# Layer 2's routing and row stores beside its attention, row loads beside layer 3, and layer 3 as a pipeline over batches

## What is computed

```python
# layer 2, ffn: a switch layer (8 experts, capacity 256 of 4096 tokens)
probs = softmax(x @ w_switch + b_switch);  pmax, routes = probs.max(-1), probs.argmax(-1)
oh = (routes[:, None] == arange(E));       pos = (cumsum(oh, axis=0) * oh).sum(-1) - 1
keep = pos < capacity;                     slot = where(keep, routes * capacity + pos, E * capacity)
buf = zeros(...).at[slot].set(x)
y = relu(buf_e @ w1 + b1) @ w2 + b2
out = where(keep, y[slot], x) * (pmax / stop_gradient(pmax))
# layer 3, attn: a selective state-space scan (16 states), then layernorm and a projection
delta = softplus(x @ W_delta.T);  B, C = x @ W_B.T, x @ W_C.T;  A = -exp(A_log)
h = h * exp(delta_t * A) + (delta_t * x_t) * B_t;   y_t = sum_n h * C_t
ctx = (layernorm(y) * gamma + beta) @ W_ctx.T * scale
# layer 3, ffn: 8 gated experts with the best 2 of 8, and 2 shared ones
```

## Time and profile before

| what | value |
|---|---|
| runs | 3924.53, 3929.08 and 3936.21 us, median 3929.08 |
| profiled execution | 3926.07 us, its span 3924.7 us |
| PE busy | 2991.2 us, 76% |
| DVE busy | 2349.8 us, 60% |
| ACT, POOL busy | 1477.4 and 814.9 us |
| mean granted PE clock | 0.8 of full speed |
| layer 2's attention ends at | 3075.0 us |
| layer 3 begins at about | 3242 us |

### The profile page before, as it was taken

The page is one execution under the profiler, slowest core; times in us unless marked ns, Lnnn a source line. Parts: engine busy times, 40 slices in busy tenths (PEclk is TensorE's granted clock), DMA queues, the critical chain, the costliest instruction groups (busy, mean ns, idle before and its releaser), DMA issues.

```text
span 3924.7 us, 47435 instructions
## 1 busy us (share of the span) xinstructions
PE 2991.2 (76%) x18187; PEld 2107.0 (54%) x18187; DVE 2349.8 (60%) x4533; ACT 1477.4 (38%) x3673; POOL 814.9 (21%) x468
## 2 busy tenths in 40 slices
PE   4877776777775869999999999688888246676676
PEld 2555454555543756666666666456555134444444
DVE  3587787788677235656566666333333217777776
ACT  1333443443343004545545454233323014444444
POOL 0032223222234201222222222100000331221221
PEclk9788888888887657989998999676677567787787
DMA  1000010001000420000000000100000030000000
GB/s 47 18 33 33 23 34 33 23 23 39 28 33 33 138 73 1 1 1 1 1 1 1 1 1 1 39 7 4 6 6 5 22 85 3 3 3 5 3 3 5
DMA packets 55346, 80.35 MB, mean 20 GB/s; under 512 B 4688, under 2 KB 38480, under 8 KB 54608
## 3 DMA queue, kind: packets, MB, share of 16 engines
q1 hardware_dynamic: 50896, 72.07, 5.6%
q0 software_dynamic: 2048, 4.20, 0.3%
q10 hardware_dynamic: 2176, 1.05, 0.1%
HBM read 68.12 MB, written 8.65 MB: 20 GB/s over the span
## 4 chain that ended last, share of the span: by engine, by line
PE 52%; DVE 29%; ACT 6%; POOL 5%; issue 5%; DMA 1%; POOLq 1%; SPq 0%; DVEq 0%; ACTq 0%
DVE h L1289 7%; PE psum L415 5%; PE psum L455 5%; PE psum L282 4%; DVE mx L1174 3%; PE psum L523 3%; PE psum L527 3%; DVE h L1281 3%; PE psum L435 2%; PE psum L683 2%; POOL h L2047 2%; PE psum L722 2%; PE psum L643 2%; POOL h L2036 2%; PE psum L534 2%
## 5 line engine op out<-in xcount | busy, mean ns | idle before, releaser
L2047 POOL TENSOR_TENSOR h<-h,Crep 128x1024 f32<-128x1024 f32 x128 | 352.9, 2763 | 947.1 <-DVE h L1289 947.1
L2017 POOL TENSOR_TENSOR pr<-pr,rsum 128x512 f32<-128x512 f32 x192 | 241.9, 1260 | 937.6 <-DVE rsum L1131 937.6
L1289 DVE TENSOR_TENSOR_SCAN h<-dA,h 128x1024 f32<-128x1024 f32 x128 | 363.6, 2845 | 0.7
L1774 ACT ACTIVATE pt<-psum 128x1024 f32<-128x1024 f32 x192 | 190.2, 1019 | 434.0 <-PE psum L534 434.0
L683 PE MATMUL psum<-h,pack_wf 128*128 128x256 f32 x1024 | 293.8, 442 | 56.7 <-POOL h L2047 56.7
L1174 DVE TENSOR_REDUCE mx<-psum 128x4 f32<-128x1024 f32 (+1 forms) x192 | 225.2, 1213 | 104.9 <-PE psum L532 104.9
L683 PEld LDWEIGHTS psum<-h,pack_wf 128*128 128x128 f32 x1024 | 223.6, 228 | 112.2 <-POOL h L2047 68.3
L1731 ACT ACTIVATE pr<-psum,nb 128x256 f32<-128x256 f32 (+1 forms) x512 | 208.4, 417 | 170.3 <-DVE nb L1123 169.6
L2036 POOL TENSOR_TENSOR h<-h,Crep 128x1024 f32<-128x1024 f32 x64 | 150.9, 2358 | 522.6 <-DVE h L1366 522.6
L415 PE MATMUL psum<-kT,qT 64*128 64x256 f32 (+1 forms) x1024 | 249.1, 381 | 3.3 <-ACT pr L1731 3.3
L1281 DVE TENSOR_TENSOR h<-dtu,psum 128x512 f32<-128x512 f32 x256 | 163.6, 679 | 105.6 <-PE psum L695 105.6
(11 more groups left out here) (338 smaller groups left out, 5984.7 us busy)
## 6 DMA issues: line engine op xcount, KB each, us to landing
Crep<-c_rows SPq DMA_DIRECT2D x64, 512.0 KB, 3.7
w1r<-m_w SPq DMA_DIRECT2D x32, 256.0 KB, 3.2
w2r<-m_w SPq DMA_DIRECT2D x32, 256.0 KB, 3.0
pack_wf<-wf SPq DMA_DIRECT2D x1, 3192.0 KB, 10.5
slots<-xn SPq DMA_DIRECT2D x16, 128.0 KB, 1.8
w1s<-s_w SPq DMA_DIRECT2D x8, 256.0 KB, 2.6
w2s<-s_w SPq DMA_DIRECT2D x8, 256.0 KB, 3.1
out<-X SPq DMA_DIRECT2D x16, 128.0 KB, 1.8
```

The lines of the kernel that those rows point to most:

```text
L1289: ve.e.tensor_tensor_scan(flat(h), flat(k.dA[c][r]), flat(h), 0.0, ALU.mult, ALU.add).then_inc(*k.set("scanned", 0, b, g, c))
L2017: po.e.tensor_tensor(p3, p3, bcast(k.rsum[u % 3][:, 0:len(heads)], P * (q + 1), 2), ALU.mult).then_inc(*k.set("normed", l, b, u))
L2047: po.e.tensor_tensor(h[:, :, :], h[:, :, :], k.Crep[n % 3][:, :, :], ALU.mult).then_inc(*k.set("hC", 0, b, g, c))
```

## The change

Layer 2:
- `slots` is zeroed by 12 DMAs at the start of layer 1 (before: 4 DMAs for the experts' part at the start of layer 2, and own rows by 16 stores). `po_pre2` and `sp_own_rows` are gone.
- The routing is part of `ve_pre2`, batch by batch, with the running totals in `run`; two small matmuls of the one-hot matrix are put at slot 21 of `pe_pre2`. Its small instructions work on 2 tiles instead of 32.
- POOL stores the rows of a batch (2 indirect DMAs) as soon as its slots are known.
- All 8 experts have weight and row buffers of their own, loaded ahead; PE runs the first matmuls of expert e before the second of e-1.
- The rows are loaded in layer 3, 2 indirect DMAs a batch, two turns ahead, and added in `ve_pre3` by one scaled add for each tile.

Layer 3 is a pipeline of 18 turns. Turn t has `inner` and `moe` of batch t, the four scan groups (`states`) of batch t-1, `post` of batch t-2 and `pre` of batch t+1. B and C are stored as 32 rows in DRAM (`bc_rows`) and spread by 8 DMAs of 512 KB a batch into one `Brep` and one `Crep` buffer for each group; the split, PE's spreading, and ACT's copies of C are gone. DVE makes `dtu*B` as one instruction of 1024 columns from SBUF.

```diff
+def pe_inner3(k, b):
+    pe, w, xnT = k.pe, k.w, k.xnT[b % 2]
+    yield 0
+    bk = pe_take(k, 3)
     pe.wait_ge(*k.at("xnT", 3, b))
+    pe.e.matmul(bk[0:2 * NS, 0:L], w["w_bc3"], xnT[:, :], start=True, stop=True)
+    pe.e.matmul(bk[:, L:2 * L], w["w_delta"], xnT[:, :], start=True, stop=True).then_inc(*k.set("dt", 3, b))
+def pe_states3(k, b):
+    for g in range(4):
+        yield STATES_AT[g] + 9
+        pe.wait_ge(*k.at("hC", 3, b, g))
...
+        for n in range(NG):
+            i = pe.e.matmul(bk, k.w["ident"], k.h[g][:, n, :], start=g == 0 and n == 0, stop=g == 3 and n == NG - 1)
+    yield 21
+    bk = pe_take(k, 2)
+    pe.wait_ge(*k.at("onehot", b))
+    pe.e.matmul(bk[:, 0:QT * E2], w["upto"], k.ohb[:, :], start=True, stop=True)
+    pe.e.matmul(bk[:, QT * E2:2 * QT * E2], w["onesb"], k.ohb[:, :], start=True, stop=True).then_inc(*k.set("totals", b))
+def ve_inner3(k, b):
+    yield 1.5
+    ve.wait_ge(*k.at("dt", 3, b))
+    ve.e.tensor_copy(k.bcrow[b % 2][:, :], bk[0:2 * NS, 0:L]).then_inc(*k.set("crow", 3, b))
...
+def ve_states3(k, b):
+    for g in range(4):
+        at, h = STATES_AT[g], k.h[g]
+        yield at
+        ve.wait_ge(*k.at("dtu", 3, b))
+        ve.wait_ge(*k.at(f"b_spread{g}", b))
+        if b:
+            ve.wait_ge(*k.at("summed", 3, b - 1, g))
+        ve.e.tensor_tensor(h[:, :, :], bcast(k.dtu[b % 2][:, :], NG, 1), k.Brep[g][:, :, :], ALU.mult).then_inc(*k.set("dbu", 3, b, g))
+        yield at + 1.5
+        ve.wait_ge(*k.at("dA", 3, b, g))
+        ve.wait_ge(*k.at("dbu", 3, b, g))
+        ve.e.tensor_tensor_scan(flat(h), flat(k.dA[g][:, :, :]), flat(h), 0.0, ALU.mult, ALU.add).then_inc(*k.set("scanned", 3, b, g))
 def ve_pre3(k, b):
+    ve.wait_ge(*k.at(f"gathered{b % 3}", b))
+    for q in range(QT):
+        n, x = b * QT + q, k.X[:, b * QT + q, :]
+        i = ve.e.scalar_tensor_tensor(x, k.got[b % 3][:, q, :], k.scl[:, n:n + 1], x, ALU.mult, ALU.add)
+def po_states3(k, b):
     po = k.po
+    for g in range(4):
+        po.wait_ge(*k.at("scanned", 3, b, g))
+        po.wait_ge(*k.at(f"c_spread{g}", "states3", b))
+        po.e.tensor_tensor(k.h[g][:, :, :], k.h[g][:, :, :], k.Crep[g][:, :, :], ALU.mult).then_inc(*k.set("hC", 3, b, g))
+def sp_spread3(k, b, g):
+    sp.wait_ge(*k.at(f"c_stored{b % 2}", 3, b))
+    for n, (t, name) in enumerate(((k.Brep[g], f"b_spread{g}"), (k.Crep[g], f"c_spread{g}"))):
+        if b:
+            sp.wait_ge(*(k.at("hC", 3, b - 1, g) if n else k.at("dbu", 3, b - 1, g)))
+        rows = bcast(k.bc_rows[b % 2, n * NS + g * NG:n * NS + (g + 1) * NG, :], P, 0)
+        sp.e.dma_start(t[:, :, :], rows).then_inc(*(k.set(name, "states3", b, by=16) if n else k.set(name, b, by=16)))
...
+def turn3(k, t, pre, inner, moe, states, post):
+    T = TURN[3]
+    merge((post(k, t - 2), 0, T, T) if post is not None and 0 <= t - 2 < NB else None,
+          (states(k, t - 1), 0, T, T) if 0 <= t - 1 < NB else None,
+          (inner(k, t), 0, T, T) if inner is not None and t < NB else None,
+          (moe(k, t), 0, T, T) if moe is not None and t < NB else None,
+          (pre(k, t + 1), 0, T, T) if pre is not None and t + 1 < NB else None)
```

More of the change, by code:

```diff
@@ new lines, in pe_moe @@
+def pe_moe(k, b):
+    pe, w, xnT, B = k.pe, k.w, k.xnT[b % 2], k.bank
+    for q in range(QT):
+        at = EXPERTS_AT[q]
+        was = (b, 0) if q else (b - 1, 1) if b else None
+        yield at
+        xl = xnT[:, q * P:(q + 1) * P]
+        pe.wait_ge(*k.at("xnT", 3, b))
+        if was is not None:
+            pe.wait_ge(*k.at("hs_up", *was))
+            pe.wait_ge(*k.at("hT3", *was))
+        for wt, bk, tail in (("x_w1", B[0], B[2][:, 0:P]), ("x_w3", B[1], B[5][:, 0:P])):
+            pe.e.matmul(bk[:, :], xl, w[wt][:, 0:512], start=True, stop=True)
+            pe.e.matmul(tail, xl, w[wt][:, 512:], start=True, stop=True).then_inc(*k.set("w13", b, q, wt))
+        yield at + 12
+        pe.wait_ge(*k.at("hs", b, q))
+        for ch in range(5):
+            o = B[0][:, ch * P:(ch + 1) * P] if ch < 4 else B[2][:, 0:P]
+            i = pe.e.transpose(o, k.hs[:, ch * P:(ch + 1) * P], w["ident"])
+        i.then_inc(*k.set("hs_turned", b, q))
+        yield at + 15
+        pe.wait_ge(*k.at("hT3", b, q))
+        if was is not None:
+            pe.wait_ge(*k.at("x_moe", *was))
+        for ch in range(5):
+            i = pe.e.matmul(B[6][:, 0:P], k.hT3[:, ch, :], w["x_w2"][:, ch, :], start=ch == 0, stop=ch == 4)
+        i.then_inc(*k.set("w2", b, q))
@@ L709, in pe_states @@
     i.then_inc(*k.set("y_out", b))
[L712 to L751, removed]
 def pe_experts0(k):
@@ new lines, in ve_experts2 @@
+    for ex in range(E2 + 1):
+        if ex < E2:
+            s = ex % 2
+            ve.wait_ge(*k.at("b_turned", ex))
+            if ex >= 2:
+                ve.wait_ge(*k.at("hidden2", ex - 2, 1))
+            ve.e.tensor_copy(k.bT[s][:, :], k.bank[s][:, 0:CAP]).then_inc(*k.set("bT", ex))
+        if ex:
+            e = ex - 1
+            s = e % 2
+            ve.wait_ge(*k.at("output2", e))
+            if e >= 2:
+                ve.wait_ge(*k.at(f"w1r{s}", "y_stored", e - 2))
+            ve.e.tensor_tensor(k.yy[s][:, :, :], halves(k.bank[6 + s][:, 0:CAP]), bcast(w["s_b2"][:, e, :], QT, 1), ALU.add).then_inc(*k.set("yy", e))
@@ L2012, in po_divide @@
+            if j % 2:
+                i.then_inc(*k.set("h2", ex, j // 2))
 def po_divide(k, l, b, u):
@@ L2069, in po_gather @@
-def po_gather(k):
-    po = k.po
-    part = NT // 4
-    for s in range(2):
-        po.wait_ge(*k.at(f"w1r{4 + s}", "y_stored", E2 - 2 + s))
-    po.wait_ge(*k.at("scattered"))
-    for i in range(NT):
-        po.e.indirect_dma_start(out=k.XN[:, i, :], out_offset=None, in_=k.rows,
-                                in_offset=bass.IndirectOffsetOnAxis(ap=k.sloti[:, i:i + 1].bitcast(U32), axis=0)).then_inc(
-            *k.set(f"gathered{i // part}", by=16))
+    po.wait_ge(*k.at("slot_ids", b))
@@ L2385, in layer2 @@
         k.ve.e.memset(v[:, :, :, 8:9], 1.0)
+    k.ve.e.memset(k.run[:, 0, :], 0.0)
     sp_layer2(k)
```

877 lines of the change are left out of this document (395 added, 482 removed).

## The result

| what | value |
|---|---|
| before, 4 runs | median 3929.01 us (3924.53 to 3936.21) |
| after, 4 runs | median 3805.79 us (3802.48 to 3814.69) |
| ratio | 0.9688, 95% interval 0.9666 to 0.9711 |
| predicted | 3771 us, range 3700 to 3850 |
| profiled execution of after | 3807.4 us, its span 3805.8 us |

The account below looks back on a forecast made before the run. Bounds: 171 us of almost no overlap after layer 2's attention, and in layer 3 a chain through DVE, POOL and PE. 3926.1 - 117 (gap) + 14 (layer 2) - 55 (layer 3) = 3768; median 3.0 higher, 3771 us; range 3700 to 3850.

Parts of the forecast that it names:

- layer 2's attention: Routing instructions added to DVE there mostly fill idle time; `oh` and `ohb` delay `mx`, first two batches lack cover: +14 us.
- gap: Stretch from layer 2's attention to layer 3's first `xnT`: routing and row stores hidden, experts overlapped; 171.0 to 54.3 us, -117.
- Hold-ups: Layer 3: DVE instructions wanting SBUF twice wait out POOL's product behind each scan, 4.7 us a turn in all.
- the walk: Stepping through the order of one layer 3 turn with assumed durations, to place collisions and waits.
- Behind the second: layernorm pieces and `lT`: 0.6: Layer 3, behind a turn's second scan: DVE loses 0.6 us to POOL's product, on layernorm pieces and `lT`.
- Behind the first ... 1.6: Layer 3, behind a turn's first scan: two copies, then `he` held up 1.6 us, half otherwise spent waiting for ACT.
- Waits: Layer 3, a turn: 2.4 us waiting for PE and ACT, plus 2.4 for PE's lower clock.
- Row loads: 0: Layer 3's two row loads a turn fall in POOL's idle time between turns and cost 0.
- rival C: Layer 3: row loads hold up POOL, a turn's first product up to 2.1 us late; 3803 us, chance 6%.
- B: Rival: layer 3's turn stays near a present batch, PE's path at lower clock; turn 41.1, 3825 us, chance 23%.
- A: Rival: layer 3's DVE and POOL collisions are hidden, the 4.7 us go; turn 32.8, 3701 us, chance 12%.
- D: Rival: layer 3's 8 spreads queue one after another; at 7 us each the turn is 56, 4049 us, chance 4%.

Follow-up runs that it names:

- e9: Changed kernel with layer 3's schedule undone, one batch at a time as before, rows still loaded and added batch by batch: 3819.6 us.
- e1: Changed kernel with PE's sum of layer 3's fourth group issued in the next turn, behind `inner` and the first expert products: 3798.3 us.
- e10: Kernel of e5 with layer 3's four products by C on DVE and DVE's gated products, states copy and `lT` later: 3696.3 us.
- e3: Changed kernel with POOL's product by C in layer 3 covering 2 of 256 columns, not a usable version: 3700.8 us.
- e5: Changed kernel with the fourth sum issued late on PE and row loads moved between POOL's products of group 0 and 1: 3756.9 us.
- e12: Kernel of e10 with all eight products by C a batch of layer 0 also on DVE, none on POOL: 3666.3 us.

## Why the prediction was right or wrong

The time lay in the range and on the forecast's side, 35 us off. Against the two profiled executions (3926.1 and 3807.4), term by term (turn 0 ends where the first product by B begins, turn 15 with its fourth scan):

| term | predicted | measured |
|---|---|---|
| layers 0 and 1, up to layer 2 | 0 | +6.5 |
| layer 2's attention | +14 | about 0 |
| gap | 171.0 to 54.3 | 171.0 to 49.4 |
| layer 3's turn 0 | 22 | 29.8 |
| 15 turns | 562.5 | 604.9 |
| turns 16 and 17 | 39 | 40.5 |

- **The gap** was right in mechanism and near in size. Experts 39.9 for 43, but not as forecast, 40.1 of PE's work and 3 beside it: PE is busy for 34.2 us of the 39.8 from 3080.1 to 3119.9, at a granted clock of 0.93 where the experts of before had 0.84, and idle for 5.6. Landing 3.9 for 3.7, norm and turn 3.3 for 4.0. e9 shows that this term is most of the change.
- **Layer 2's attention: +14 was wrong.** From the last add of layer 1 (ended 2495.7 before, 2502.2 after) to the last of layer 2 it took 579.3 us, and 579.0 after, with DVE at 267 us for 203. `oh` and `ohb` do put `mx` off, by 0.28 us in 14 of the 16 turns (0.62 from `v` to `mx` for 0.34), and in the first two turns it is 4.3 and 1.1 us: some 9 us that the stretch does not show. PE was busy for 8.3 us less in it (469.0 for 477.3), at a granted clock of 0.71 for 0.69, which would make up for them; no run tests it. The other twelve kernels, all with the new layer 2, take 568.1 to 578.7 us for the same stretch.
- **The 6.5 us before layer 2** were put at 0 and are in part open. Layer 0 ends within 1 us of before; layer 1 takes 1193.5 us for 1187.8, and 1190.0 to 1193.5 in the twelve other kernels. Since there is but one trace of before, this is 2 to 6 us that may be the change's, whose 12 zeroing stores stand in layer 1, or may not. The rest is scatter: the profiles of eleven programs that are the same up to there (the changed kernel, e1 to e10) put the end of layer 2's attention anywhere from 3072.8 to 3084.5. So of the small differences below 12 us between runs none is leaned on without the turn's length beside it.
- **Layer 3's work, 27.7 us a turn, was right** (27.6; e3 gives 27.4, from 353.6 us busy in 451 and a turn of 34.9). One part of its sum is off: eight instructions of 0.28 to 0.41 are 2.8 us rather than 2.5.
- **Hold-ups, 4.7 predicted, 5.5 measured.** Where the walk placed them they were: the product by B is bimodal, at 1.2 and 3.40, as its 2.2 asked for. The step that failed is "Behind the second: layernorm pieces and `lT`: 0.6". What stands behind the second scan is the norm of the states, whose pair took 2.61 for 0.7. Behind the third "`he` comes first and POOL waits" holds for turn 1 alone; from then on `he` waits 0.88 us for ACT, POOL is first, and `he` takes 1.90. "Behind the first ... 1.6" did not come, since `he` there arrived 3.2 us late, after POOL was through. It came in e5, when that wait had gone. The Trainium skill, SBUF — State Buffer, section Who interferes with whom, counts `tensor_scalar` among the instructions that can enter a two-port mode and then contend with GpSimd. The pair at 2.61 and `he` at 1.90 agree, both being `tensor_scalar` within SBUF, and the walk should have asked it of every instruction behind a scan.
- **Waits, 4.8 predicted (2.4 for PE and ACT, 2.4 for PE's lower clock), 7.9 measured.** This is the larger miss, 3.1 of the 3.8 us between the sum, 37.2, and 41.0. "Waits for PE and ACT in the same walk: 2.4" took the last state sum at its short time. PE runs it in 3.78 us in every full turn, at a granted clock of 0.50 and behind 2.6 us of idle time, and `inner`, `bcrow`, the first expert products and ACT's exponentials all queue behind it. Idle time is not all that it takes: in nine turns of e3 the same sum stands behind 0.1 to 0.5 us of it and still takes 3.2 to 3.8 us. e5 took the sum out of the way and the turn fell by 3.1 us at the same mean clock in mid-layer (0.75), so the new order as a whole is worth those 3.1. How they divide between the sum's place and its time is open, since the moved sum also runs in 1.9 to 2.0 us, and the prediction's 2.4 for the clock is neither confirmed nor refuted. An estimate from these rows: at 1.99 in its old place it would have freed 1.8 of the 2.18 us that `bcrow` waits. No run has it so.
- **"Row loads: 0"** came out right, by luck. They took 1.79 us on POOL for 0.95, rival C's mechanism, and put the product of group 0 off by 0.8 us; but PE was not yet ready for it. What the prediction didn't see is that they are issued only 6 us before DVE wants them, which used up what a faster turn gave (e1 against e5).
- **Spreads: 0** held, and so did their share, 0.35 by the estimate and 0.35 to 0.37 in the windows. A spread by SP lands in 5.8 or 7.0 us, not 3.7, in bursts at a DMA share up to 0.99, and nobody waits for it. Even e10 with its turn of 34.1 has no wait for one.
- **The ends**: turn 0 was 7.8 us too short in the sum. It was put at half a batch and has the whole chain of the first experts.
- **The rivals.** By the marks set beforehand ("over 40 (B)") B's figure came true: 41.0 us for 41.1. It had 23%, and its total, 3825, is nearer to the 3805.8 than the forecast's 3771. That the total came nearer to the forecast than the turn did is luck: the +14 and the gap's 5 us went the other way. B's mechanism, all of PE's path at the lower clock, is not what is seen: one of the four sums takes 3.78 us, one 3.2, two 1.9 to 2.0. A, C and D did not come; the floor that A named (32.8) is not far from what e10 reached by other means (34.1).

## What to carry to other kernels

After pipelining stages on engines that run in order, take one turn and write down the idle time ahead of each instruction of the fullest engine: a long piece of work that is ready but not urgent (here a sum of 3.78 us) belongs behind the short pieces that others wait for. A POOL product of this size beside a busy DVE is not free: count up to 2.2 us for the next DVE instruction that has two inputs in SBUF or is a `tensor_scalar` within SBUF, and move the product to DVE (1.22 us) where it also leads a wait, but not everywhere, as e12 shows. Two edits that each measure nothing may be worth 49 us together, so a load that is issued shortly before its use has to be moved before the rest is judged.
